# Expert slots of 256 rows of one expert in place of pairs of 128-row slots, in a kernel of RWKV mixing and top-2 experts on one core

## The reference

```python
scores = einsum('btd,ed->bte', x, gate_w)            # x is layer-normed
topk_scores, topk_idx = top_k(scores, 2)
topk_probs = softmax(topk_scores)
h12 = einsum('btd,ehd->bteh', x, w12)                # 128 -> 2 * 256 for each expert
hidden = silu(h12[..., :256]) * h12[..., 256:]
expert_out = einsum('bteh,edh->bted', hidden, w3)    # 256 -> 128
y = sum over the two picked experts of prob * expert_out
```

## Time and profile before

| what | value |
|---|---|
| time, median of 3 runs | 349.81 us (347.94 to 350.32) |
| span of the profiled execution, first to last instruction | 381.7 us |
| PE busy in it | 279.6 us (73%) |
| DVE busy | 249.1 us (65%) |
| POOL busy | 215.2 us (56%) |
| ACT busy | 196.8 us (52%) |

### The profile page before, as it was taken

One profiled execution on the slowest core, in us unless ns is written; L12 is line 12 of the kernel. 1 busy time (PEld: TensorE's weight loads), 2 busy tenths in 40 slices (PEclk: granted clock), 3 DMA queues, 4 the chain that ended last, 5 costly groups with the idle time before them and its releaser, 6 DMA issues.

```text
span 381.7 us, 6770 instructions
## 1 busy us (share of the span) xinstructions
PE 279.6 (73%) x1697; PEld 217.7 (57%) x1698; DVE 249.1 (65%) x790; ACT 196.8 (52%) x413; POOL 215.2 (56%) x227
## 2 busy tenths in 40 slices
PE   0685899989979699695943317987887898887720
PEld 0233475748575566464622106987887887887610
DVE  3089998998899959883544701646654654645675
ACT  3445688776867556644610022646664664645300
POOL 5142465277886768858747730454565565465482
PEclk9996699998989679968795586999999999999955
DMA  8900000001011001111111213232222222232774
GB/s 287 396 12 2 0 2 27 2 36 43 34 42 42 28 33 45 35 44 42 54 35 58 86 49 79 55 82 65 68 80 70 68 78 71 62 85 61 249 255 186
DMA packets 22406, 29.08 MB, mean 76 GB/s; under 512 B 4317, under 2 KB 15583, under 8 KB 22128
## 3 DMA queue, kind: packets, MB, share of 16 engines
q1 hardware_dynamic: 14832, 13.45, 12.1%
q0 software_dynamic: 4352, 8.47, 6.7%
q10 hardware_dynamic: 3200, 6.90, 4.8%
HBM read 15.09 MB, written 12.14 MB: 71 GB/s over the span
## 4 chain that ended last, share of the span: by engine, by line
issue 25%; DVE 23%; POOL 8%; another core or an unknown queue 8%; PE 7%; ACT 5%; DMA 4%; ACTq 4%; SPq 3%; DVEq 1%; POOLq 0%
POOL rows_d L416 4%; ACTq L615 3%; DVE rden L886 3%; DVE st L825 3%; ACT w_up L618 3%; PE p_up L799 2%; DMA o_all<-res_d 2%; DVE num L880 2%; DVE den L876 2%; DVE spots L974 1%; PE p_f L726 1%; DVE mv L832 1%; DMA res_d<-yo,result_row 1%; ACT xgT L609 1%
## 5 line engine op out<-in xcount | busy, mean ns | idle before, releaser
L441 POOL DMA_INDIRECT res_d<-yo,result_row x72 | 71.2, 990 | 71.7 <-DVE yo L1071 53.0
L416 POOL DMA_INDIRECT rows_d<-rows,pos x64 | 67.3, 1052 | 22.6 <-issue 22.6
L799 PE MATMUL p_up<-xgT,w_up 128*128 128x128 f32 x576 | 71.8, 279 | 0.0
L799 PEld LDWEIGHTS p_up<-xgT,w_up 128*128 128x128 f32 x576 | 68.8, 196 | 0.0
L1056 DVE SCALAR_TENSOR_TENSOR gate_h<-th,p_up 128x512 f32<-128x512 f32 x36 | 24.8, 688 | 46.3 <-issue 24.1
L618 ACT ACTIVATE w_up<-w_exp 128x512 f32 x72 | 41.6, 623 | 14.3 <-issue 13.4
L714 PE MATMUL p_up<-ysum,w_sb 128*128 128x512 f32 x64 | 36.4, 678 | 5.0 <-POOL ysum L395 5.0
L603 ACT ACTIVATE th<-p_up 128x512 f32<-128x512 f32 x36 | 21.4, 595 | 30.9 <-remote 13.8
L726 PEld LDWEIGHTS p_f<-wfv_half,kk 128*128 128x128 f32 x256 | 34.3, 210 | 5.2 <-issue 4.9
L726 PE MATMUL p_f<-wfv_half,kk 128*128 128x128 f32 x256 | 35.1, 294 | 0.0
L789 PE MATMUL p_tr<-ident,xg 128*128 128x128 f32 x72 | 14.9, 289 | 21.0 <-ACT xgT L609 10.9
(11 more groups left out here) (153 smaller groups left out, 568.2 us busy)
## 6 DMA issues: line engine op xcount, KB each, us to landing
xg<-rows_d SPq DMA_DIRECT2D x72, 65.0 KB
o_all<-res_d SPq DMA_DIRECT2D x16, 256.0 KB, 6.8
w_exp<-experts ACTq DMA_DIRECT2D x1, 3072.0 KB, 17.1
x_all<-x SPq DMA_DIRECT2D x10, 256.0 KB, 2.3
out<-x_all ACTq DMA_DIRECT2D x8, 256.0 KB, 2.4
x_all<-x SPq DMA_DIRECT2D x1, 1536.0 KB, 16.4
res_d<-yo,result_row POOLq DMA_INDIRECT x72
rows_d<-rows,pos POOLq DMA_INDIRECT x64
```

Source lines behind the costliest of these rows:

```text
L416: pool.indirect_dma_start(out=rows_d[:, :], out_offset=bass.IndirectOffsetOnAxis(ap=row, axis=0), in_=rows_of[is_last(c)][:, t, k, :], in_ ...
L441: pool.indirect_dma_start(out=res_d[:, :], out_offset=bass.IndirectOffsetOnAxis(ap=row, axis=0), in_=yo[u][:, n, :], in_offset=None, bound ...
L799: mm = pe.matmul(p_up[u % 2][:, n, h * P:(h + 1) * P], w_up[u % 2][:, n, h * P:(h + 1) * P], xgT[u % 2][:, n, :], start=True, stop=True)
```

## The change

A turn now works on 256 rows of one expert. There are (8192 - 8) // 256 + 8 = 39 slots of 256 rows, again enough for the worst split, and 39 turns. A slot has one set of weights, so ACT copies one 128x512 block a turn, and the up step is 4 products of 256 columns against the same weights. The `rows_d` of a slot are fetched by one transfer that gives each partition two neighbouring rows. Each expert's region gets 256 pad rows in place of 128, the idle region has 256 rows in place of 1024. `p_up` now holds the gate half in one bank and the other half in the other. The table is made for 39 slots, with one more operation: a `min` that keeps all idle slots on the one idle region.

```diff
-SLOTS = TOKENS * TOPK // P + E
-IDLE = E
+SLOTS = (TOKENS * TOPK - E) // SR + E          # SR = 2 * P
-PAIRS = SLOTS // 2
...
         def fill_pads(eng, experts):
                 n = eng.value_load(total_i[0:1, e:e + 1], min_val=0, max_val=TOKENS)
-                eng.dma_start(rows_d[bass.ds(n + e * REGION, P), :], pad[:, :]).then_inc(S["pad_filled"], 16)
+                eng.dma_start(rows_d[bass.ds(n + e * REGION, SR), :].rearrange("(p n) w -> p n w", n=2), pad_twice)\
+                    .then_inc(S["pad_filled"], 16)
...
             def load(q, r, u):
-                for n in range(2):
-                    sp.dma_start(xg[u][:, n, :], rows_d[bass.ds(first_row[n], P), :]).then_inc(S[f"xg_loaded{u}"], 16)
+                sp.dma_start(xg[u][:, :, :], rows_d[bass.ds(row, SR), :].rearrange("(p n) w -> p n w", n=2))\
+                    .then_inc(S[f"xg_loaded{u}"], 16)
...
             def expert_weights(q, _, u):
-                for n in range(2):
-                    first_col = act.snap(loaded[n], min_val=0, max_val=(E - 1) * EW)
-                    act.activation(w_up[u % 2][:, n, :], w_exp[:, bass.ds(first_col, 2 * H)], ACT.Copy)
+                first_col = act.snap(loaded, min_val=0, max_val=(E - 1) * EW)
+                act.activation(w_up[u % 2][:, :], w_exp[:, bass.ds(first_col, 2 * H)], ACT.Copy)
...
             def up(q, _, u):
-                for n in range(2):
-                    for h in range(2 * H // P):
-                        mm = pe.matmul(p_up[u % 2][:, n, h * P:(h + 1) * P], w_up[u % 2][:, n, h * P:(h + 1) * P],
-                                       xgT[u % 2][:, n, :], start=True, stop=True)
+                for h in range(2 * H // P):
+                    mm = pe.matmul(p_up[u % 2][:, h // 2, (h % 2) * SR:(h % 2 + 1) * SR], w_up[u % 2][:, h * P:(h + 1) * P],
+                                   xgT[u % 2][:, :, :], start=True, stop=True)
...
             # the table
-            dve.scalar_tensor_tensor(out=slot_row[:, :], in0=slot_e[:, :], scalar=float(REGION), in1=slot_first[:, :],
-                                     op0=ALU.mult, op1=ALU.add).then_inc(S["table_row"], 1)
+            link(dve.scalar_tensor_tensor(out=slot_first[:, :], in0=slot_e[:, :], scalar=float(REGION), in1=slot_first[:, :],
+                                          op0=ALU.mult, op1=ALU.add))
+            dve.tensor_scalar(slot_row[:, :], slot_first[:, :], float(E * REGION), None, ALU.min).then_inc(S["table_row"], 1)
```

More of the change, by code:

```diff
@@ L121, in build @@
         xgT = [sb(f"xgT{n}", [P, 2, P]) for n in range(2)]
-        w_up = [sb(f"w_up{n}", [P, 2, 2 * H]) for n in range(2)]
-        th = sb("th", [P, 2, H]); gate_h = sb("gate_h", [P, 2, H])
-        hid = [sb(f"hid{n}", [P, 2, H // P, P]) for n in range(2)]
+        w_up = [sb(f"w_up{n}", [P, 2 * H]) for n in range(2)]
+        th = sb("th", [P, CT]); gate_h = sb("gate_h", [P, CT])
+        hid = [sb(f"hid{n}", [P, H // P, 2, P]) for n in range(2)]
         yo = [sb(f"yo{n}", [P, 2, D]) for n in range(BUFS)]
@@ L221, in rounds @@
             lags = [lag for _, lag in steps]
-            last_round = (PAIRS - 1 + min(lags) - (BUFS - 1)) // BUFS
+            last_round = (SLOTS - 1 + min(lags) - (BUFS - 1)) // BUFS
             def turn(r, u):
                 for step, lag in steps:
-                    if not isinstance(r, int) or 0 <= r * BUFS + u - lag < PAIRS:
+                    if not isinstance(r, int) or 0 <= r * BUFS + u - lag < SLOTS:
                         off, place = divmod(u - lag, BUFS)
@@ L234, in rounds @@
                     turn(r, u)
-            for i in range((last_round + 1) * BUFS, PAIRS + max(lags)):
+            for i in range((last_round + 1) * BUFS, SLOTS + max(lags)):
                 turn(i // BUFS, i % BUFS)
+        pad_twice = pad[:, :].rearrange("p (o w) -> p o w", o=1).to_broadcast([P, 2, ROW])
         def fill_pads(eng, experts):
@@ L268, in _, with first_row @@
             fill_pads(sp, range(0, E, 2))
[L270 to L275, removed]
+            row_number = sp.alloc_register("first_row")
+            def first_row(q):
+                sp.load(row_number, slot_row[0:1, bass.ds(q, 1)])
+                return sp.snap(row_number, min_val=0, max_val=E * REGION)
             sp.wait_ge(S["late_wait_ready"], 1)
@@ L284, in load @@
             def load(q, r, u):
-                first_row = first_rows(q)
+                row = first_row(q)
                 if isinstance(q, int) and q < EARLY:
@@ L302, in _ @@
                 written = [nc.values_load(last_scatter[0:1, k, u:u + 1], engines=(mybir.EngineType.SP,), min_val=32,
-                                          max_val=32 * PAIRS // BUFS) for u in range(BUFS)]
+                                          max_val=32 * ROUNDS) for u in range(BUFS)]
                 for u in range(BUFS):
@@ L452, in _ @@
             for u in range(BUFS):
[L453 removed]
+                pool.wait_ge(S[f"scattered{u}"], 32 * len(range(u, SLOTS, BUFS)))
         @block.scalar
@@ L593, in _ @@
             fill_pads(act, range(1, E, 2))
-            loaded = [act.alloc_register(f"first_col{n}") for n in range(2)]
+            loaded = act.alloc_register("first_col")
             act.wait_ge(S["table_w"], 1)
@@ L781, in _ @@
             pe.wait_ge(S["experts_in"], 16)
-            loaded = [pe.alloc_register(f"first_col{n}") for n in range(2)]
+            loaded = pe.alloc_register("first_col")
             def turn_rows(q, r, u):
-                after(pe, f"xg_loaded{u}", r * 32 + 32)
+                after(pe, f"xg_loaded{u}", r * 16 + 16)
                 after(pe, "xgT_ready", q)
```

46 lines of the change are left out of this document (24 added, 22 removed).

## The result

The changed kernel takes 359.1 us (median of four runs, 358.15 to 361.78) where the kernel before takes 348.9 beside it: a ratio of 1.0318 with a 95% interval of 1.0267 to 1.0368, so 10 to 11 us slower. The forecast was 355.5, 5.8 us slower.

What follows compares the result with a forecast made beforehand. The prediction took PE to bound the kernel in dense turns of 2.90 us. It added +6.8 us for the turns and -1.0 between the stages to 349.8, giving 355.6, forecast as 355.5 us, range 345.5 to 360.

Steps and rivals of the forecast that it cites:

- Slower, by the count of turns: Second stage: 39 turns of 2.85 us in place of 36 of 2.90, +6.8 us, ends +5.9 and +8.7.
- The up products: PE in a turn: eight passes of 256 columns at 0.218 us replace sixteen of 128, gaining 0.05 us a turn.
- Rival two: PE's up products: weight loads pace narrow passes but not wide ones, so turns fall to 2.54 us; 343.5 us, chance 0.04.
- The remote waits: Stalls in the profiled span were taken as the profiler's own cost, 32.9 us together, absent from timed runs.
- Rival one: PE's late signals are real and go with the number of passes: 332 us, or 347.7 if a third is real; chance 0.14.
- Rival three: The timed turn is longer than 2.90 us, say 3.23, by something both kernels share: 358.5 us, chance 0.10.
- Between the stages: From expert totals to first load: shorter table, added min, saved second issue and fills sum to -1.0 us, ends -1.3 and +0.5.
- Rival four: Gains between the stages are larger, for instance the first load waits for SP alone: 3 us, 353.6 us, chance 0.20.
- The landing of the fills: Between the stages: the larger pads land under POOL's last dispatches, put at no cost.
- The issue of the fills: SP's four pad fills ahead of its first load: between the old issue time and twice it, up to +2.0 us.
- The gain of the shorter table: DVE's four table operations shrink to 312 elements, saving 1.0 us; less the added min, -0.5 us.
- The saved second issue: The first slot no longer waits for a second load to be issued: -0.57 us.

Runs made afterwards that it cites:

- e3: The changed kernel with 36 slots in place of 39, without the three slots these inputs leave unused: 354.4 us, ratio 1.0192 to the kernel before.
- e0: The kernel before, unedited, profiled a second time: 349.0 us, profiled span 346.9 us.
- e2: The changed kernel with its up products cut to 128 columns again, the rest as changed: 361.79 us, ratio 1.0382 to the kernel before.
- b2: The kernel before with only the changed kernel's pad fills of 256 rows added: 352.52 us, ratio 1.0102 to the kernel before.
- e1: The changed kernel with a pad tile two rows wide, so fills go in 1040-byte pieces, not 520: 354.08 us, ratio 1.0143 to the kernel before.
- x1: The kernel before with the eight expert counts read into registers by one load on each engine, not one by one: 345.72 us, ratio 0.9915.
- a1: The changed kernel with all eight pad fills issued by ACT and none by SP: 356.78 us, ratio 1.0247 to the kernel before.
- x2: The changed kernel with both the two-row pad tile and the expert counts read by one load: 353.91 us, ratio 1.0179 to the kernel before.

## Why the prediction came out as it did

**Slower, by the count of turns: right, in size too.** The prediction put +6.8 us on 39 turns of 2.85 in place of 36 of 2.90; the stretch from first to last tanh grew by 6.5, with turns of 2.84 and 2.90. That all three added turns cost their full length holds for the reason given, that the used ones grow as well. What the prediction used to show that idle turns are not free was half of it: e3 shows that 3.5 of 8.5 us of the three at the end are covered.

**The up products: right.** 0.218 us was read off the line between a 128 and a 512 pass, and 0.216 measured; a gain of 0.06 us a turn where 0.05 was summed. Rival two, narrow passes paced by their weight loads, falls with it: a wide pass takes nearly twice a narrow one, 0.216 against 0.111 us.

**The remote waits: right.** Taking them out of the sum was the step with the largest stake (32.9 us), and it rested on arithmetic alone. e0 confirms it: the span is 346.9, and the turns are 2.90. Where the stalls were put was right too: the disturbed trace is 23.0 us longer from first to last tanh (123.83 against 100.80) and 9.1 from the totals to the first transposes, where the arithmetic had 23.8 and 9.1. Rival one falls with e0 and e2. The reason given, records that cannot be written fast enough, is not confirmed: e0 wrote the same records without a stall. Why that execution was disturbed stays open. Rival three falls as well, as the undisturbed turn is 2.90 us; that its 358.5 lies nearer to the measured time than the forecast is chance.

**Between the stages: the step that failed.** The term was -1.0 us, with +0.5 as its upper end; it measured +4.4. Rival four, larger gains there, falls with it. Four things were in the term.

*The landing of the fills* was put at nothing: "the landing of the larger pads lies under POOL's last dispatches". For the mark that POOL sets at the end of them (`late_rows`) that is so: it stands right behind the landing of the last dispatch in both traces. But it stands 13.0 us after the totals before and 15.4 after, so the dispatches, too, land later by 2.4 us. And the early loads do not wait for the mark; they go out among the fills, on the same 16 engines. The first load took 5.55 us in place of 1.96, +3.6 us. b2 has the fills without the rest of the change: its first load lands 3.4 us later than before, half of that by a later issue, and the run is 3.6 us longer. e1, with the same bytes in half the pieces, takes back the later issue and most of the longer landing (3.06 us). The sum priced the issue of the fills and not their passage.

*The issue of the fills* was bounded by the old size and twice that. An issue takes 0.55 to 0.63 us now and 0.33 to 0.37 before; the first load goes out 1.0 us later after the totals (9.04 against 8.01). This lies inside the bound of +2.0.

*The gain of the shorter table,* -0.5, exists and is worth nothing: the first slot's row is written 4.76 us after the totals instead of 5.68, but SP reads it at 8.5. The prediction believed that the table came after SP by 0.9 us. Its estimate of 1.2 us a fill was right (four take 4.9 us in e0), but it took the table's time from the disturbed trace as it stood, 219.29 or 7.8 us after the totals there, and the table had been delayed in it as well. In e0 SP is the later one, by 1.56 us, which x1 turned into a gain. That SP alone sets the first load was the first reason of rival four, and true, though the gain it expected did not come with this change.

*The saved second issue,* -0.57, shows: from the landing of the first load to the first transposes it was 0.78 us before, while the second half of the slot was still on its way, and it is 0.14 now, -0.64.

Behind the first transposes lies what the sum did not hold at all. From there to the first up products it is 1.67 us now instead of 2.19, but these ran from 224.17 to 226.95, 2.78 us for what takes 1.73 later, at a granted clock of 0.50 (1.2 GHz) from 222.50 to 224.17 and of 0.64 up to 227.15 (the mean of 0.50 up to 226.29 and 1.00, 2.4 GHz, from there), after PE had been idle for 5.45 us waiting for the load:

```profile
222.50:224.17 1.67, 1.11 (x4) 0.73 (x5) 0.00 (x0) 0.38 (x1) 0.10 (x1) 0.50 0.00 0
224.17:227.15 2.98, 2.98 (x11) 2.41 (x11) 0.00 (x0) 0.38 (x1) 0.00 (x0) 0.64 0.51 131
```

Before, PE waited 1.75 us there, the clock was 1.00, and they took 1.79. Together +0.5.

**The sum, mended:** +6.5 for the turns, +4.0 ahead of the first transposes and +0.5 behind them are 11.0 us, against 10.2 by the medians and 11.1 by the ratio; the spans differ by 9.5, with the 1.8 us of the first stage and the 0.4 at the end in it. The forecast's +5.8 is short by 4.4 to 5.3, of which the passage of the fills is 3.6. The direction and the main term were right for the reason given. That 359.1 still lies within the range, at the upper end of the sum itself (359.0), is in part luck: that end allowed for up products that gain nothing and for fills that are issued in twice the time, and neither came; the excess came from a term that had been put at nothing.

**What stays open.** Whether it is the engines' time for each piece, the repeated read of one row of the pad, or the writes to memory that makes two 520-byte pieces dearer than one of 1040 was not separated; e1 changed all three. That the first load pays for engines shared with all queues is shown by a1; how much it also waits behind the fills of its own queue is not. And even mended, by e1 or x2, the 256-row slots remain 1.4 to 1.8% above the kernel before; the three used turns that the rounding to 256 rows adds have to be paid in any version, and 0.06 us a turn does not pay for them.

## What to carry to other kernels

When independent tiles are regrouped into larger ones of one owner, first count how many turns the rounding adds for the real inputs, and multiply by the dense turn: 3 x 2.85 us stood here against 36 x 0.06. Then price the side transfers that grow with the tile by their pieces and by who shares the DMA engines while they pass, not by the time it takes to issue them; "it lies under X" must be asked of every wait, not of the last one. And where a profiled span lies far above the timed runs, work out what the timed runs must look like, but do not read from that trace which of two engines is later: the table stood 2.1 us late in it.

## What the runs showed of the hardware that was not expected

- The time of a packet depends on what else is under way. The packets of ACT's queue, nearly all fill pieces of 520 bytes, take 25 ns each before (14.4 us over 576 packets), 49 ns in the changed kernel (53.6 over 1088), 33 ns in a1. Those of 1040 bytes in e1 take 48 ns, at a DMA share of 0.70 from 210 to 221 us where the changed kernel has 1.09, so size and jam are not told apart.
- The issue of a fill went with its pieces and not with its bytes: 0.33 to 0.40 us for 128 pieces, of 520 bytes before or of 1040 in e1, and 0.47 to 0.69 for 256 pieces of 520 in the changed kernel and b2.
- Engines that show a share of 1.09 over 11 us moved 158 GB/s in them, where the first 15 us of the same trace have 334 at a share of 0.87; the share told of the jam, the rate did not.
- A wait of 5.45 us for a load was followed by a granted clock of 0.50 on the products behind it, a wait of 1.75 us at the same place by 1.00. Between them the length of the wait alone does not tell: after 2.78 us in e1 the clock fell to 0.50 at 221.57, 2 us after PE had begun again, and after 2.90 us in x2 it stayed at 1.00.
- One profiled execution of an unchanged kernel can be 35 us longer than the next, with the excess laid down as waits that end "remote".
